# Flamingo block with a top-2 expert layer on one core: value matmuls turned round into float32 column groups, and a tile's front end moved by a quarter tile

## What is computed

```python
xn, xfn = layer_norm(layernorm(x)), layer_norm(ctx)          # with gains and shifts
q, k, v = xn @ Wq + bq, xfn @ Wk + bk, xfn @ Wv + bv         # 16 heads of 8
w = softmax(q @ k.T / sqrt(8))                               # 128 x 77 for each head
x = x + tanh(g_xattn) * (w @ v)                              # heads side by side
logits = layernorm(x) @ w_router                             # 8 experts, the top two, softmax over them
h = square(relu(einsum('nc,ecd->ned', layernorm(x), w1)))
x = x + tanh(g_ffn) * sum over the two experts of prob * (h @ w2)
```

## Time and profile before

| | |
|---|---|
| median of 3 runs | 432.58 us (431.52 to 435.71) |
| the profiled execution | 432.84 us |
| its span in the trace | 431.0 us |
| mean granted TensorE clock | 0.761 |
| busy: PE, DVE, ACT, POOL | 309.2, 291.7, 224.9, 221.8 us |

### The profile page before, as it was taken

The page is one execution under the profiler, slowest core; times in us unless marked ns, Lnnn a source line. Parts: engine busy times, 40 slices in busy tenths (PEclk is TensorE's granted clock), DMA queues, the critical chain, the costliest instruction groups (busy, mean ns, idle before and its releaser), DMA issues.

```text
span 431.0 us, 9014 instructions
## 1 busy us (share of the span) xinstructions
PE 309.2 (72%) x2664; PEld 261.7 (61%) x2664; DVE 291.7 (68%) x956; ACT 224.9 (52%) x490; POOL 221.8 (51%) x261
## 2 busy tenths in 40 slices
PE   0502693779399849885997869885888599699566
PEld 0301472667388738874786748774777488587455
DVE  5524744875577787868785787877887678847432
ACT  1210353556356765676565646764576467665222
POOL 8601353664566555755573458545754565665100
PEclk9965555555559975998598958995999589769869
DMA  2346019001831075206530382229211821050140
GB/s 51 100 87 93 2 44 142 5 2 42 143 125 75 33 116 157 106 28 105 159 119 8 78 170 75 75 75 159 96 75 57 146 97 78 27 198 2 47 174 24
DMA packets 29314, 36.57 MB, mean 85 GB/s; under 512 B 5849, under 2 KB 22874, under 8 KB 29274
## 3 DMA queue, kind: packets, MB, share of 16 engines
q1 hardware_dynamic: 28474, 35.05, 33.1%
q0 software_dynamic: 512, 1.06, 0.9%
q10 hardware_dynamic: 288, 0.00, 0.0%
HBM read 23.14 MB, written 2.23 MB: 59 GB/s over the span
## 4 chain that ended last, share of the span: by engine, by line
PE 39%; DVE 23%; issue 13%; DMA 11%; SPq 5%; POOL 4%; ACT 3%; DVEq 1%; POOLq 0%; ACTq 0%
PE y L533 10%; DMA qs<-q_lo 8%; PE ab L455 6%; PE s L477 5%; SPq L313 4%; DVE u L947 3%; DVE negm L831 3%; PE c L493 3%; DVE xn L782 3%; PE h L524 2%; PE ab L437 2%; DMA gb<-gates_scratch 2%; PE h L526 2%; PE h L525 2%; DVE x L867 2%
## 5 line engine op out<-in xcount | busy, mean ns | idle before, releaser
L1079 POOL TENSOR_TENSOR p_lo<-p,p_hi 77x512 f16<-77x512 f32 x128 | 147.8, 1158 | 109.9 <-ACT p L681 109.7
L831 DVE TENSOR_REDUCE negm<-ab 128x4 f32<-128x308 f32 x128 | 58.9, 470 | 72.7 <-PE ab L455 69.8
L455 PE MATMUL ab<-ks,qs 96*128 96x312 f32 x128 | 62.8, 495 | 39.8 <-DMA qs<-q_lo 27.4
L680 ACT ACTIVATE p_hi<-s 77x512 f16<-77x512 f32 x128 | 74.8, 585 | 31.2 <-PE s L477 30.9
L533 PE MATMUL y<-w2s,hs 128*128 128x128 f32 x512 | 74.2, 293 | 6.1 <-ACT hs L688 6.0
L477 PEld LDWEIGHTS s<-qs,ks 104*77 104x77 f32 x512 | 70.1, 194 | 10.9 <-issue 4.8
L681 ACT ACTIVATE p<-s 77x512 f32<-77x512 f32 x128 | 74.8, 584 | 0.0
L533 PEld LDWEIGHTS y<-w2s,hs 128*128 128x128 f32 x512 | 67.5, 206 | 8.1 <-ACT hs L688 7.4
L477 PE MATMUL s<-qs,ks 104*77 104x128 f32 x512 | 72.0, 280 | 0.2 <-ACT p L681 0.2
L455 PEld LDWEIGHTS ab<-ks,qs 96*128 96x128 f32 x128 | 31.1, 244 | 47.0 <-issue 33.9
L688 ACT ACTIVATE hs<-u 128x512 f32<-128x512 f32 x64 | 40.2, 628 | 31.3 <-DVE u L947 29.1
(11 more groups left out here) (100 smaller groups left out, 503.7 us busy)
## 6 DMA issues: line engine op xcount, KB each, us to landing
gb<-gates_scratch SPq DMA_DIRECT2D x16, 768.0 KB, 4.2
qs<-q_hi SPq DMA_DIRECT2D x16, 256.0 KB, 5.7
gb<-gates_scratch SPq DMA_DIRECT2D x8, 512.0 KB, 3.6
ks<-k_hi SPq DMA_DIRECT2D x64, 39.0 KB
x_sb<-in_x_dram SPq DMA_DIRECT2D x8, 256.0 KB, 6.7
qs<-q_lo SPq DMA_DIRECT2D x8, 256.0 KB, 6.9
x_res<-in_x_dram SPq DMA_DIRECT2D x8, 256.0 KB, 6.8
out_dram<-y_out SPq DMA_DIRECT2D x8, 256.0 KB, 5.8
```

The lines of the kernel that those rows point to most:

```text
L455: nc.tensor.matmul(p[:, 0:J * NP].rearrange("t (i n) -> t i n", n=NP), qs[0:QR, par, c, T * j:T * j + T], ks[0:QR, par, c, :, NP * j:NP * ...
L680: nc.scalar.activation(p_hi[:, c, :], src, ACT.Exp).then_inc(hi_done, 1)
L831: nc.vector.tensor_reduce(negm[:, :, c], bank_ab[bank][:, 0:J * NP].rearrange("t (i n) -> t i n", n=NP)[:, :, 0:N], AX.X, ALU.max, negate= ...
L1079: nc.gpsimd.tensor_tensor(p_lo[:, c, :], p32[:, c, :], p_hi[:, c, :], ALU.subtract).then_inc(lo_done, 1)
```

## The change

Value matmuls are turned round: the weights are now 32 columns of `vs` for one head (8 values and a one, padded with zeros; even heads of a pair in the first 16 columns and odd ones in the second), and the 128 columns of the float32 exponentials `p32` move. The four heads of a group c go to four different groups of 32 output partitions of `bank_c`; groups 0 and 1 are added up in the same place, as are 2 and 3. So there is one exponential instead of two, no low part on POOL, and values stay float32 and are not split. The result now has heads on partitions: ACT copies it (`evacuate_heads`), PE turns it back by two transposes (`turn_heads`), and DVE divides straight from that bank. The heads come out in another order, which the addition of the residual undoes by its access pattern. `vs` is cleared at the start on POOL.

The front end moves one slot earlier: statistics to slot 1, roots, normalising and transposes to slot 2, projections, their splitting and stacking to slot 3, for the tile `third`. On SP the stack DMAs move from slot 0 to slot 3, behind that slot's maxima and ahead of that slot's gate broadcast; the load moves to the head of slot 0. On DVE the first step of `attended` moves behind `routed`.

```diff
--- before.py
+++ after.py
 AB_USES = [
-    (-1, "turn2"), (0, "s1c2"), (-1, "route2"), (0, "s1d2"), (1, "k"), (0, "mT2"), (1, "q"), (0, "s1a3"),
-    (0, "s1b3"),
-    (-1, "turn3"), (0, "s1c3"), (-1, "route3"), (0, "s1d3"), (1, "v"), (0, "mT3"), (-1, "gates"), (1, "s1a0"),
-    (1, "s1b0"),
-    (0, "turn0"), (1, "s1c0"), (0, "route0"), (1, "s1d0"), (1, "mT0"), (1, "s1a1"), (1, "s1b1"),
-    (0, "turn1"), (1, "s1c1"), (0, "route1"), (1, "s1d1"), (1, "mT1"), (2, "ctxT"), (1, "s1a2"), (1, "s1b2"),
-    (2, "xT"),
+    (-1, "turn2"), (0, "s1c2"), (-1, "route2"), (0, "s1d2"), (-1, "o3"), (0, "mT2"), (0, "s1a3"), (0, "s1b3"),
+    (-1, "turn3"), (0, "s1c3"), (-1, "route3"), (0, "s1d3"), (0, "o0"), (1, "v"), (0, "mT3"), (-1, "gates"),
+    (1, "s1a0"), (1, "s1b0"),
+    (0, "turn0"), (1, "s1c0"), (0, "route0"), (1, "s1d0"), (0, "o1"), (1, "mT0"), (2, "ctxT"), (1, "s1a1"),
+    (1, "s1b1"), (2, "xT"),
+    (0, "turn1"), (1, "s1c1"), (0, "route1"), (1, "s1d1"), (0, "o2"), (2, "k"), (1, "mT1"), (2, "q"),
+    (1, "s1a2"), (1, "s1b2"),
...
 MAXP = ["hi", "lo"]
-POST = ["summed", "recip", "scaled", "x1", "stats", "moments", "normed"]
+POST = ["recip", "x1", "stats", "moments", "normed"]
...
     NC = H // CH
-    VC = HD * PARTS + 1
+    VC = 2 * HD
+    VT = 2 * VC
     SCALE = float(HD) ** -0.5
...
             def step(i, par, loop=False):
                 for j, near, nxt, third, ffn in slots(i, par, loop):
-                    if j == 0 and nxt:
-                        stack_k(i + 1, 1 - par, 0, loop)
+                    if j == 0 and third and (loop or i > -2):
+                        load(i + 2, par, loop)
                     if near[2]:
                         max_rows(*near[2])
                     if j == 0 and nxt:
-                        stack_k(i + 1, 1 - par, 1, loop)
-                        stack_q(i + 1, 1 - par, 0, loop)
-                        stack_q(i + 1, 1 - par, 1, loop)
-                        if not loop and i < 1:
-                            unit_rows(1 - par)
                         load_rows(i + 1, 1 - par, loop)
-                    if j == 0 and third and (loop or i > -2):
-                        load(i + 2, par, loop)
+                    if j == 3 and third:
+                        stack_k(i + 2, par, 0, loop)
+                        stack_k(i + 2, par, 1, loop)
+                        stack_q(i + 2, par, 0, loop)
+                        stack_q(i + 2, par, 1, loop)
+                        if not loop and i < 0:
+                            unit_rows(par)
                     if j == 1 and exists(i - 2, loop):
                         store(i - 2, par)
...
                 n = G * s + j
                 m = NC * n + c
                 if c == 0:
-                    pe.wait_ge(split_v, at(SPLIT, s, "lo"))
+                    bank, k = ab(s, "v")
+                    pe.wait_ge(v_done, s + 1)
+                    pe.wait_ge(ab_taken[bank], k)
+                    if not loop and n == 0:
+                        pe.wait_ge(v_ones, ONES)
                     if loop or n > 0:
-                        pe.wait_ge(post_d, at(POST, n - 1, "recip"))
-                pe.wait_ge(lo_done, m + 1)
+                        pe.wait_ge(o_taken, n)
+                pe.wait_ge(p_done, m + 1)
+                r = T * (c // 2)
                 for i in range(J):
-                    h, k = NC * i + c, T * i
-                    for part in (p_hi, p_lo):
-                        mm = nc.tensor.matmul(bank_c[:, VC * h:VC * h + VC], part[:, c, k:k + T],
-                                              vs[:, par, j, h, :], start=(c == 0 and i == 0 and part is p_hi),
-                                              stop=(part is p_lo), skip_group_check=True)
+                    mm = nc.tensor.matmul(bank_c[VT * i:VT * i + VT, r:r + T], vs[:, par, j, NC * i + c, :],
+                                          p32[:, c, T * i:T * i + T], start=(c == 0), stop=(c % 2 == 1),
+                                          skip_group_check=True)
                 mm.then_inc(pv_done, 1)
+
+            def turn_heads(s, par, j, loop=False):
+                pe.wait_ge(o_taken, G * s + j + 1)
+                p, ready = claim(s, f"o{j}", loop)
+                for r in range(2):
+                    mm = nc.tensor.transpose(p[:, T * r:T * r + T], oT[:, T * r:T * r + T], ident[:, :])
+                mm.then_inc(ready, 1)
 
...
                         scoresT(*near[0], 1, loop)
+                    if near[-1]:
+                        turn_heads(*near[-1], loop)
                     if e[0] is not None:
                         hidden(sf, pf, e[0], loop)
-                    if j == 0 and nxt:
-                        project_keys(nxt[0], loop)
+                    if j == 3 and third:
+                        project_keys(third[0], loop)
                     if e[1] is not None:
                         hidden(sf, pf, e[1], loop)
                     if near[0]:
...
                     if near[0]:
                         values(*near[0], 0, loop)
-                    if j == 0 and nxt:
-                        project_queries(nxt[0], loop)
+                    if j == 3 and third:
...
                         output(sf, pf, e[0], loop)
                     if j == 1 and exists(i - 1, loop):
                         gates_turn(i - 1, loop)
-                    if j == 3 and third:
+                    if j == 2 and third:
...
                         scores(*near[3], 1, loop)
                     if near[0]:
                         values(*near[0], 1, loop)
-                    if j == 3 and third:
+                    if j == 2 and third:
...
                 bank, n = ab(s, "v")
                 if loop or s >= 2:
                     act.wait_ge(pv_done, NC * G * (s - 1))
+                else:
+                    act.wait_ge(v_ones, ONES)
                 act.wait_ge(ab_ready[bank], n)
...
+                for odd, done in enumerate((v_done, ab_taken[bank])):
+                    k = VC * odd
+                    nc.scalar.activation(vs[:, par].rearrange("n b (m o) k -> n o (b m) k", o=2)[:, odd, :, k:k + HD],
+                                         bank_ab[bank][0:N, :].rearrange("n (m o d) -> n o m d", o=2, d=HD)[:, odd],
+                                         ACT.Copy, scale=col(GX, N)).then_inc(done, 1)
+
+            def evacuate_heads(s, par, j):
+                act.wait_ge(pv_done, NC * (G * s + j) + NC)
+                nc.scalar.activation(oT[:, :], bank_c[:, 0:2 * T], ACT.Copy).then_inc(o_taken, 1)
 
             def evacuate_turned(s, par, j, loop=False):
...
                 src = bank_s2[c % 2][0:N, :]
-                nc.scalar.activation(p_hi[:, c, :], src, ACT.Exp).then_inc(hi_done, 1)
                 nc.scalar.activation(p32[:, c, :], src, ACT.Exp).then_inc(p_done, 1)
...
             def attended(s, par, j, loop=False):
 
                 n = G * s + j
-                dve.wait_ge(pv_done, NC * n + NC)
-                view = bank_c[:, 0:VC * H].rearrange("t (h v) -> t h v", v=VC)
-                nc.vector.tensor_reduce(o[:, :].rearrange("t (h d) -> t h d", d=HD),
-                                        view[:, :, 0:HD * PARTS].rearrange("t h (d a) -> t h d a", a=PARTS),
-                                        AX.X, ALU.add).then_inc(post_d, 1)
+                bank, k = ab(s, f"o{j}")
+                view = bank_ab[bank][:, 0:VC * H].rearrange("t (h v) -> t h v", v=VC)
+                dve.wait_ge(ab_ready[bank], k)
                 nc.vector.reciprocal(rden[:, :].rearrange("t (h o) -> t h o", o=1),
-                                     view[:, :, HD * PARTS:VC]).then_inc(post_d, 1)
+                                     view[:, :, HD:HD + 1]).then_inc(post_d, 1)
                 yield
                 dve.wait_ge(post_d, at(POST, n, "recip"))
-                nc.vector.tensor_tensor(o[:, :].rearrange("t (h d) -> t h d", d=HD),
-                                        o[:, :].rearrange("t (h d) -> t h d", d=HD),
+                nc.vector.tensor_tensor(o[:, :].rearrange("t (h d) -> t h d", d=HD), view[:, :, 0:HD],
                                         rden[:, :].rearrange("t (h o) -> t h o", o=1).broadcast_to([T, H, HD]),
-                                        ALU.mult).then_inc(post_d, 1)
+                                        ALU.mult).then_inc(ab_taken[bank], 1)
                 yield
                 if j == 0:
                     dve.wait_ge(res_in[par], landed(s, par))
                     if loop or s >= 2:
                         dve.wait_ge(y_added, s - 1)
-                dve.wait_ge(post_d, at(POST, n, "scaled"))
-                nc.vector.tensor_tensor(x1[:, par, j, :], x_res[:, par, j, :], o[:, :], ALU.add).then_inc(post_d, 1)
+                dve.wait_ge(ab_taken[bank], k)
+                nc.vector.tensor_tensor(x1[:, par, j, :].rearrange("t (i r e) -> t i r e", i=J, r=2),
```

(34 more changed lines are left out.)

59 lines of the change are left out of this document (10 added, 49 removed).

## The result

The changed kernel takes 505.45 us (median of 4 runs, 504.38 to 506.68) beside 432.05 us for the kernel before: a ratio of 1.168, interval 1.161 to 1.176. The forecast was 479 us in a range of 428 to 512, with a chance of 0.82 on slower. The time lies inside the range, 26 us above the forecast.

A forecast was written before the change was run, and what follows sets the result against it. The prediction took PE to set the time in three slots of four. Its terms, 22 + 14 - 14 - 5 + 25 + 4 = +46 us on 432.84 us, gave 479 us, range 428 to 512.

The forecast's parts named there:

- What SP is moved past: SP, slot 3: gate broadcast queues behind 15 stack DMAs, so DVE's `u` waits in slot 0; +25 us (+10 to +35).
- Value matmuls: PE: four float32 matmuls a group, partly overlapping, +0.26 us a group over 84 groups; +22 us (+8 to +57).
- groups fully side by side: Rival on PE: column groups run together, value term 8 instead of 22, gates still late; 465 us, chance 0.2.
- Heads turned back: PE: two transposes a slot plus a wait for the logits copy, 0.68 us in 21 slots; +14 us (+6 to +19).
- What is added on PE there is paid in full: PE sets the time in three slots of four (2, 3, 0), so work added there costs its full length.
- DVE and POOL lightened: Slot 1: gates come earlier and the `q_lo` wait goes, -2 us in 7 tiles; -14 us (-28 to -4).
- Front end a quarter earlier: Steady transposes and projections only change slots; the 15 us starting wait shrinks; -5 us (0 to -12).
- the shift doesn't help at the start: Rival: the front end isn't earlier at the start; 484 us, inside the range, no separate chance given.
- Start: POOL clears `vs` ahead of the first norms, 3.7 us, with two small fills; +4 us (bound 0).
- not slower: Rival: values near free, late gates not met, slot 2 at full clock; 426 us, chance 0.2.

The follow-up runs named there:

- experiment 1: Changed kernel with SP's gate broadcast of slot 3 issued ahead of the 15 stack DMAs, not behind them; 441.13 us, ratio to before 1.011.
- experiment 8: As experiment 1, but every value matmul writes output partitions 0 to 31, one column group, attention's output left out; 531.65 us, ratio to before 1.221.
- experiment 5: Kernel before with only the front end one slot earlier, values unchanged, gate broadcast ahead of the stack DMAs; 429.47 us, ratio to before 0.986.
- experiment 6: As experiment 1, with `turn_heads` on PE moved behind the slot's first `hidden`; 441.26 us, ratio to before 1.010.
- experiment 4: Kernel before with only the front end one slot earlier, values unchanged, gate broadcast behind the stack DMAs; 500.23 us, ratio to before 1.153.
- experiment 7: As experiment 6, with clearing of `vs` on DVE instead of POOL and POOL's later `ks` clearing one slot later; 436.08 us, ratio to before 0.993.
- experiment 10: As experiment 7, with value group 0 directly ahead of group 1 and POOL's fills waiting for the first normalisation; 434.29 us, ratio to before 1.000.

## Why the prediction was right, and where it was off

The sign and the cause were right. The sum was near because two errors of opposite sign partly met: the forecast was +46, of which 25 for the late broadcast and 21 for all the rest; measured is +64 for the broadcast (505.45 against experiment 1's 441.13; 68 by the ratios 1.168 and 1.011) and +6 for the rest (441.13 against 434.69 for the kernel before beside it; 5 by the ratio). That they met is luck.

- **What SP is moved past: the step that was mis-sized, 25 us where it is 64.** Its first half held to 0.4 us: stack at +8.4 (forecast +8.8), broadcast issued at +19.0 (+19.2). Then three sizes were off. The landing was taken as the 4.2 us of the earlier trace rows, a median of broadcasts with no stack queued ahead; it is 8.2 behind fifteen stack transfers. Slot 3 is 11.2 us, not 12.3, so slot 0 starts earlier against the same broadcast. And I counted 5 us of a tile's wait, as if PE's other work were cover; every slot 0 pays 10.8 to 13.3. The upper bound of 35 was too low as well, since it only added a colder clock to the same landing. The wait has no cover because `u` stands at the head of DVE's queue and PE's queue follows: once both are stopped, nothing else runs. PE's clock adds to it, 0.71 in that slot against 1.00 in experiment 1: the same 96 matmuls keep PE busy for 12.0 us and not 9.3.
- **Value matmuls: direction right, decomposition wrong.** I took halves of one head in sequence with the next head beside them, 0.46 us a group. Measured are 0.36 for a group by itself and 0.57 for two in a row (318.35 to 318.92), thus 0.29 each, the figure that I had given for groups fully side by side. The price is that rival's, not mine. The `scores` matmul ahead of a group then takes 0.31 to 0.33 us to the next start, where one that has no group behind it takes 0.23 (316.66 to 316.89), and `max_turn` takes 0.20 where it took 0.11, so 0.09 three times a slot. Together about 0.7 us a slot, where the forecast had 1.04. The Trainium skill, TensorE: Matmul & The Clock Gate, Part 3, speaks for column tiles running together, and experiment 8 agrees (0.96 against 0.36 us, 2.7 times for four groups). The toll at a change of mode of which the Trainium skill speaks (TensorEngine Tiling (Array Packing), Key Properties) can be the 0.09 us going in; no run here shows that a drain is its cause.
- **Heads turned back: 0.68 forecast, 0.87 measured** in a slot, and the cause as given. On PE, from the scores to the first `hidden`:

```profile
321.11 0.43 PE L469 MATMUL s<-qs,ks 104*77 104x128 f32 x4
322.08 0.41 PE L497 MATMUL ab<-ident,oT 128*128 128x128 f32 x2 [0.54 <-DVE logits L886]
322.24 0.48 PE L526 MATMUL h<-x_hi,w_lo 128*128 128x512 f32 x1
```

- **"What is added on PE there is paid in full": wrong.** Values and heads add 1.6 us of PE time to a slot. Between experiments 5 and 1 slot 3 grows by 0.29, slot 2 by 0.85 and slot 0 by 0.95, and a late slot grows from 8.72 to 9.81. Two waits of PE gave way to the new work. One stands in each of these slots: the next `scores` matmul started 0.51 us behind `route` (275.86 to 276.37) and now starts 0.29 behind it (320.57 to 320.86). Two lines of the kernel before, and the later one of after:

```profile
275.86 0.37 PE L508 MATMUL ab<-wr,xT 128*128 128x8 f32 x2
276.37 0.42 PE L455 MATMUL ab<-ks,qs 96*128 96x312 f32 x1
320.86 0.41 PE L447 MATMUL ab<-ks,qs 96*128 96x312 f32 x1
```

  The other is the 0.92 us for which the projection of queries waits on `k_lo`. I had read it and moved it into slot 3 with the projection. Experiment 5 still has it there; the changed kernel, with the heads ahead of it on PE, has not. In this order:

```profile
177.46 1.10 PE L437 MATMUL ab<-xnT,wq 128*128 128x512 f32 x2 [1.00 <-DVE k_lo L803]
313.87 1.13 PE L429 MATMUL ab<-xnT,wq 128*128 128x512 f32 x2
```

  From experiment 5 to experiment 1, which is values and heads on top of the shift, the time grows by 11.7 us, 3.9 of it at the start; the forecast for this had been 22 + 14 - 14 + 4 = 26. This, more than the price of a group, is why the rest came to 6 instead of 21.
- **DVE and POOL lightened:** slot 1 forecast 2 us shorter, measured 1.1 to 1.8 in four steady tiles. Line 880 of before (line 869 of after) now takes 0.31 to 0.35 us in all 32 places, as forecast. The turned values alone are worth 2.5 us there (14.24 in experiment 5, 11.79 in 1): DVE's busy time in the slot goes from 12.8 to 8.0.
- **Front end a quarter earlier:** -5 forecast, -6 measured (429.47 against 435.24), and by luck, since the 5 us at the start did not come. The wait there is 15.1 us as before (15.0), the first transpose of experiment 5 is at 74.81 against 74.18. That rival (the shift doesn't help at the start) was right. The steady slots, which I took as even, gain: slot 0 falls by 2.0 and slots 2 and 3 rise by 1.0 together.
- **Start:** +4 forecast for the clearing of `vs`, +3.8 measured at the first norm (8.82 to 12.62) and +4.5 at the first transpose.

The rival *not slower* had its mechanism right (slots fall to what PE needs, once the gates aren't late) and its price wrong: with its condition made true by hand the kernel takes 441 us, not 426, because the cold slot 2 did not speed up and the late slots without a front end each grow by 1.1 us.

## What to carry to other kernels

When transfers are moved on a queue, list what is now issued behind them and who waits for it, and price both halves: the issue time of everything ahead, and a landing that is longer than the median measured with an empty queue. A wait at the head of an in-order engine on which PE depends is paid in full; count no cover unless the engines' queues show work ahead of the wait. And where a window shows PE busy for less than its length, added PE work first fills the gap: slots 2, 3 and 0, which look alike on the busy line, had 0, 1.2 and 1.1 us of room, and even slot 2 grew by only half of what was added. And look at what a wait is for: one that moves with its instruction can vanish behind the new work.

## What the runs showed that I had not expected

- Four column groups of float32 matmuls run together, both halves of each: eight records of 128 columns in 0.36 us, 0.96 when they share one group. At the half clock sixteen take 1.01 us to the next start (295.66 to 296.67), against 0.57 at the full one.
- A copy or a scalar operation on DVE beside a clearing on POOL lasts until the clearing ends. In the changed kernel the copy of `wk` takes 2.32 us, 0.30 before. On DVE's timeline:

```profile
9.01 2.32 DVE L964 COPY wk<-wk_in 96x128 f32<-96x128 f32 x1 [2.46 <-DMA wv<-in_L_xattn_bv_dram]
```

and on POOL's:

```profile
7.66 3.59 POOL L1093 MEMSET vs<- 77x4096 f32 x1
```

  It ends at 11.33 and the clearing at 11.25. The Trainium skill, SBUF — State Buffer, Who interferes with whom, calls the port pair that both share an exclusive lock, and this agrees. Not every DVE operation is held: a `BATCH_NORM_STATS2` of `x_sb` takes 0.27 us beside the clearing of `ks` in the kernel before, and 0.27 just ahead of it in the changed one. The 5.1 us of the first normalisation were in the kernel before already (11.57 to 16.71), unseen by me on the path of the start; one wait on POOL took 4 us out of it and 3.65 off the first transpose.
- The landing of a 768 KB broadcast depends on what is queued ahead: 4.4 to 5.0 us with no stack ahead, 6.0 to 6.6 behind twelve transfers of 39 KB, 8.1 to 8.2 behind those and three of 256 KB.
- A mean granted clock over a stretch that has no clock records says nothing. In the profile of experiment 6 the first record comes at 98.9 us, and the view gives 1.00 for all that lies ahead of it. PE's durations there are those of the half clock, the same as in the changed kernel (the record of 0.50 is there in its trace) and not the 0.39 us of a warm slot:

```profile
80.50 0.61 PE L447 MATMUL ab<-ks,qs 96*128 96x312 f32 x1
80.53 0.61 PE L447 MATMUL ab<-ks,qs 96*128 96x312 f32 x1
```

  The first line is of experiment 6, the second of the changed kernel. The same holds for the start of experiments 4, 7 and 10.
